# Gathers of an edge group are issued only when the four gathers of the group before have landed

## The reference, cut to what matters

```python
def gnn(feat, W_self, W_neigh, b, src, dst):
    msg = feat[src]                                        # one gathered row per edge
    agg = segment_sum(msg, dst, num_segments=n)
    deg = segment_sum(ones_like(dst), dst, num_segments=n)
    return feat @ W_self + (agg / maximum(deg, 1.0)[:, None]) @ W_neigh + b

def ffn(x, gamma, beta, Wr, br, W1, b1, W2, b2):
    xn = layernorm(x) * gamma + beta
    top_vals, top_idx = top_k(xn @ Wr + br, 2)
    w = softmax(top_vals)
    for e in range(8):
        h = gelu(xn @ W1[e] + b1[e])
        y += (h @ W2[e] + b2[e]) * w_full[..., e, None]
    return y

x = x + gnn(layernorm(x), ...)
x = x + ffn(layernorm(x)[None], ...)[0]
```

## Time and profile before

| | us |
|---|---|
| median of 3 runs | 1588.26 |
| lowest and highest | 1587.45 to 1598.54 |
| profiled execution, span from first to last instruction | 1546.9 |
| median less span: what lies around the span | 41.4 |

### The profile page before, as it was taken

How to read it: one execution, slowest core, us unless ns; L and a number is a source line. 1 busy time by engine, 2 the same in 40 slices (tenths; PEclk the granted TensorE clock), 3 DMA queues, 4 the chain that set the end, 5 groups by cost and what they waited for, 6 DMA issues and landing times.

```text
span 1546.9 us, 22459 instructions
## 1 busy us (share of the span) xinstructions
PE 1199.9 (78%) x6492; PEld 1041.8 (67%) x6493; DVE 867.0 (56%) x2814; ACT 426.8 (28%) x803; POOL 944.1 (61%) x1023
## 2 busy tenths in 40 slices
PE   0377988888977798989889888677858775879857
PEld 0266777867866676877778777566747764778747
DVE  6745556665564655656565565554636553545426
ACT  5412222222322332332332323213313210211111
POOL 6756656666566666566655657665665566666642
PEclk9788999999997899999999999788978897999979
DMA  9798777755454565555554555464565556656545
GB/s 335 232 297 247 244 230 239 238 166 173 152 166 124 164 190 160 181 172 171 188 182 157 181 157 164 135 191 133 165 204 157 167 158 199 201 165 222 167 139 175
DMA packets 175355, 289.69 MB, mean 187 GB/s; under 512 B 25600, under 2 KB 105344, under 8 KB 175104
## 3 DMA queue, kind: packets, MB, share of 16 engines
q1 hardware_dynamic: 124288, 156.38, 30.6%
q0 software_dynamic: 45504, 124.36, 27.3%
q10 hardware_dynamic: 5440, 7.47, 1.4%
HBM read 231.43 MB, written 56.68 MB: 186 GB/s over the span
## 4 chain that ended last, share of the span: by engine, by line
PE 33%; DVE 28%; another core or an unknown queue 21%; issue 12%; DVEq 2%; POOL 2%; DMA 1%; SPq 0%; ACT 0%; POOLq 0%; ACTq 0%
PE bank L1040 9%; PE bank L964 8%; PE bank L1066 6%; DVE agg L1311 5%; PE bank L1074 4%; DVE heap L1468 4%; DVE onehot L1257 3%; PE bank L952 2%; PE bank L993 1%; PE bank L995 1%; DMA heap<-in_x 1%; DVE nstats L1339 1%; DVE xf L1334 1%; DVE agg L1337 1%
## 5 line engine op out<-in xcount | busy, mean ns | idle before, releaser
L689 POOL DMA_INDIRECT ring<-feature_table,src_sb x760 | 742.3, 977 | 468.3 <-issue 194.6
L964 PE MATMUL bank<-ring,onehot 128*128 128x257 f32 x1552 | 404.0, 403 | 73.5 <-DMA rows<-in_x,src_sb 40.9
L964 PEld LDWEIGHTS bank<-ring,onehot 128*128 128x128 f32 x1552 | 312.1, 203 | 131.7 <-issue 83.4
L1468 DVE TENSOR_TENSOR heap<-bank,b_sb 128x512 f32<-128x512 f32 x145 | 100.1, 690 | 342.1 <-remote 249.7
L1066 PE MATMUL bank<-heap 128*128 x712 | 193.5, 418 | 60.4 <-issue 18.1
L1040 PE MATMUL bank<-row_t,heap 128*128 128x128 f32 x1424 | 195.9, 294 | 38.8 <-DVE heap L1468 19.3
L1040 PEld LDWEIGHTS bank<-row_t,heap 128*128 128x128 f32 x1424 | 186.6, 208 | 46.2 <-issue 45.0
L866 ACT ACTIVATE heap<-heap 128x512 f32<-128x512 f32 x145 | 91.6, 632 | 453.7 <-DVE heap L1468 312.7
L1066 PEld LDWEIGHTS bank<-heap 128*128 128x128 f32 x712 | 142.4, 208 | 86.0 <-issue 66.3
L1040 PE MATMUL bank<-dst_i,heap 128*128 128x128 f32 x896 | 115.8, 284 | 32.8 <-DVE heap L1468 25.9
L1257 DVE TENSOR_TENSOR onehot<-iota,target 128x512 f32<-128x512 f32 x196 | 134.3, 685 | 6.9 <-DVE xf L1328 3.5
(11 more groups left out here) (190 smaller groups left out, 1258.1 us busy)
## 6 DMA issues: line engine op xcount, KB each, us to landing
heap<-in_w SPq DMA_DIRECT2D x145, 512.0 KB
expert_out<-empty_row SPq DMA_DIRECT2D x68, 256.0 KB
ring<-feature_table,src_sb POOLq DMA_INDIRECT x760
row<-expert_rows SPq DMA_DIRECT2D x89, 128.5 KB
xf<-in_x SPq DMA_DIRECT2D x49, 128.0 KB
ff<-feature_table SPq DMA_DIRECT2D x49, 128.0 KB
expert_out<-inside SPq DMA_DIRECT2D x45, 128.0 KB
expert_out<-y_out SPq DMA_DIRECT2D x44, 128.0 KB
```

The costliest lines, as they stand in the source:

```text
L689: pool.indirect_dma_start(group_row(t, i)[:, 0:D], None, x if t < RAW else table, bass.IndirectOffsetOnAxis(src_sb[:, k:k + 1], 0)).then_i ...
L964: last = pe.matmul(bank[t % 2][:, 0:D + 1], onehot[:, q, i, :], group_row(t, i), start=(i == 0), stop=(i == GT - 1))
L1468: dve.tensor_tensor(hid[S.slot(u, 2)], hidden_b[:, :].rearrange("p (k t) -> p k t", k=HK), b1_sb[:, bass.ds(e, 1), :].rearrange("p o k -> ...
```

## The change

`gather(t)` gets one more wait. From group 7 on (t > RAW), POOL waits until all four gathers of group t-1 have landed before it issues the first gather of group t. Nothing is removed, and no other engine's program differs.

```diff
@@ gather(t), on GpSimd
                 if t >= GS:
                     pool.wait_ge(gathered[q], 16 * GT * (t // GS))
+                if t > RAW:
+                    before = t - 1
+                    pool.wait_ge(gathered[before % GS], 16 * GT * (before // GS + 1))
                 for i in range(GT):
                     k = g * GT + i
                     pool.indirect_dma_start(group_row(t, i)[:, 0:D], None, x if t < RAW else table,
```

## The result

The changed kernel takes 1737.64 us (median of 4, 1736.14 to 1741.96) against 1589.47 us: 1.0925 times as long, 95% interval 1.0893 to 1.0958, or 148 us slower. The direction was forecast, the size wasn't: 54 us were, and the range ended at 1700.

A forecast was written before the change was run, and what follows sets the result against it. No engine ran all the time; PE was busiest, gathers hidden. Chained gathers would bound the first stretch: 34 + 15 + 5 = 54 us on 1546.9, span 1601, with 41.4 around it 1642 us; range 1608 to 1700.

The forecast's parts named there:

- That gathers were hidden with a lead, and the wait makes them a chain that becomes the bound: POOL's gathers, 16.6 us ahead of PE, become a chain: group t begins when t-1 has landed, cycle 4.06 us plus landing.
- The restart of 0.3 us: On POOL, from a group's landing to the next group's first gather: 0.3 us in every cycle.
- the guess of 10: 377 to 977 us: a fifth of the 83 slots lose 0.6 us each to uneven slot lengths, +10 us.
- L of 3.7 and 3.1: Landing time from the fourth gather's start: 3.7 us from 83 to 377 us, 3.1 later; bounds 2.4 and 5.7.
- The lead of 16.6 us, used once and won back between 977 and 1377 us: POOL's lead over PE offsets 16.6 us in the first stretch, returns in the third, offsets the last stretch again.
- 0.45 us for a pair behind the gathers: Each scatter or take pair issued behind the fourth gather adds 0.45 us to the cycle.
- Late takes fall into slack and cost nothing: DVE waits some 3 us for each late take, in the third stretch's first slots, where PE has slack.
- the rival that priced them at 48 us: SP, held at 12 list ends by late scatters, delays weight loads, about 4 us each: 48 more, 1690 us; chance 0.15.
- The clock costs nothing: PE's clock sinks oftener in the added waits, at no cost while the gather chain is the bound.
- The 41.4 us around the span: Time taken to lie around the profiled span, added to 1601 us of span to give 1642.
- Its own signs: Changed kernel's profile: over half the growth in the first 44 groups, none from 977 to 1377 us.
- the rival of dearer landings: Landings take 4.0 and 3.5 us instead of 3.7 and 3.1: 53 us more, 1695 us; chance 0.12.

The follow-up runs named there:

- the run with t-2: As the change, but the new wait is for group t-2 instead of t-1: 1560.45 us against 1559.0, ratio 1.0003.
- the three partial kernels: The change with its wait only at groups 7 to 50, 51 to 135 or 136 to 195: 1652.1, 1641.45 and 1612.59 us.
- five kernels: The change (1737.64 us); landing wait first of three (1672.9), middle (1731.09); two waits, landing last (1738.06) or first (1662.57).

## Why the prediction was wrong

Point by point, by its own steps:

- **That gathers were hidden with a lead, and the wait makes them a chain that becomes the bound:** right. The waits released by a landing, the full-ring waits nearly gone, and the matmul right behind its landing in 100 groups show it, and the run with t-2, where all of this is absent, is as fast as before.
- **The restart of 0.3 us: this is the step that failed.** It was taken from POOL's start 0.27 us behind a matmul of PE and carried over to a landing. A landing with the wait in this place measured 1.14. Two things lie between. L was counted to the last packet, and the semaphore is complete 0.35 us behind it; and PE's semaphore is carried by the gather itself, 0.26 us, while the landing's stands on the extra row, 0.79. The error of 0.83 us stands in every cycle that is the bound.
- **What the sum gives with it.** With the measured restart, the prediction's own L, and neither the pairs nor the guess of 10: 44.1 x 8.59 - 294 - 16.6 = 68; 83 x 7.99 - 600 = 63; 0; 16.9 x 7.99 - 100 - 16.6 = 18 (the recorded 5 of this stretch is 4 when worked out): 150 us, and with the 41.4 again 1738, within a microsecond of what was measured. That match is luck. These slots are those of the quick profile, whose growth was 189 us, not 148: by stretch 64, 59, 26, 33 and 8. The sum fits the first two; it lacks 26 us at slots 136 to 146, about 15 in the last stretch and 8 behind it, and the 41.4 us that weren't around the span made up for them.
- **L of 3.7 and 3.1:** a little high. From the fourth gather's start to the last packet, mean of the 37 and 62 groups without a scatter behind them, it was 3.5 and 3.0 us. (The 96% of q1 stand just behind the late landing that gave the high end; during it q1 had 71, 41 and 89%.) As foreseen, the DMA share fell with the pace, from 0.74 to 0.63.
- **The lead of 16.6 us, used once and won back between 977 and 1377 us:** half right. The size was right, 17 us in the median of all groups up to 135, and so was the gain: up to 15 us in the median from 146 to 175, which took 260 us against 261. But by group 174 it was used up again, so the last stretch had none to use, and grew by 34 us and not by 18.
- **0.45 us for a pair behind the gathers:** nearly void. With a restart of 1.1 us the next group starts 4.1 us behind the fourth gather's start (mean of groups 51 to 136 without a pair), later than the 3.85 us that a pair takes. In groups 51 to 136 a cycle with a pair took 8.1 us, one without 8.0.
- **Late takes fall into slack and cost nothing:** DVE waited 11 us for two of them, and slots 136 to 146 grew by 26, of which the takes make at most about 12. Late scatters at list ends: not seen by themselves; the rival that priced them at 48 us is unlikely, since the three partial kernels leave only 11 of the 148 us, and parts of the open 14 us may be theirs.
- **The clock costs nothing:** not tried apart. The granted clock sank as foreseen, to 0.87, 0.80 and 0.90 in the first, third and last stretch against 0.93, 0.86 and 0.93, and PE's busy time rose by 53 us; in the second stretch it is 0.92 in both, so it is no cause of the 59 us there.
- **The 41.4 us around the span:** wrong, 1.7. It hid that the profiled execution was a quick one, so that the slots set beside the cycle were shorter than usual.
- **Its own signs:** the growth was to lie for more than half in the first 44 groups and to be nothing in the third stretch. It was a third of the 189 us there, and 25 us from group 136 to 176, the sign that it had named for scatters and takes.
- **Range and rivals:** the rival of dearer landings had the right form, a cycle that is longer by a constant, and the wrong term. The range left the restart at its one value and gave bounds to L alone. A second row, the landing of a DMA with an engine waiting for it on the spot, would have been needed; POOL in the kernel before offers hardly one.

## What to carry to other kernels

When a change makes a queue wait for its own transfers, write the cycle as issue + landing + restart, multiply it by all its repetitions and set it beside the slot; with a slot of 7.2 us and a cycle of 6 to 8, each tenth of a microsecond decides. The restart belongs in the sum with a bound on both sides like any other term, and must be read from a wait of the same kind and in the same place, not from the nearest semaphore. Where one of several waits in front of an instruction is the one that really holds the engine, try it first in the source: here it was worth 65 to 75 us. A window of one more item in flight (t-2 instead of t-1) made the same wait free.

## What the runs showed of the hardware

- Of several waits in front of one of GpSimd's indirect DMAs, the first in the source was carried by the DMA's own row and the others stood on one extra row ahead of it (184 groups in each of five kernels). From the complete semaphore to the start of the DMA it took 0.26 us in the first case, whether a matmul or a landing completed it, and 0.75 to 0.79 us in the second.
- The semaphore of a gather was complete 0.35 us behind its last packet. So GpSimd's next indirect DMA started 1.1 us behind the last packet, or 0.6 us with the wait first; TensorE's matmul 0.44 us behind it. The order of the three lines was worth 65 us of 1738.
- A third wait in 188 groups that was met in nearly all of them cost nothing measurable: ratio 1.0003 (0.9955 to 1.0051), and 0.30 us between two DMAs as without it.
- A gather of 131 KB had its last packet 2.4 us after its start on clear engines, and up to 6.2 us beside bursts of the other queue; over the changed kernel the median was 2.6.
